# Eight of a batch's sixteen rows of B through DMA and ScalarE instead of TensorE, and a second product with C on GpSimd

## The reference, cut to what matters

```python
xn = layernorm(x)
deltaBC = xn @ W_deltaBC.T                       # 64 + 16 + 16 columns
delta, Bmat, Cmat = split(deltaBC)
delta = softplus(delta @ W_dt.T + b_dt)          # [b, 512, 256]
deltaA = exp(delta[..., None] * A)               # [b, 512, 256, 16]
BX = delta[..., None] * Bmat[:, :, None, :] * xn[..., None]
hs = scan(h = deltaA * h + BX, along the tokens)
y = einsum('blds,bls->bld', hs, Cmat) + D * xn
ffn = for each expert: gate * (gelu(xn[top] @ W1 + b1) @ W2 + b2), added to rows top
out = x + y + ffn
```

## Time and profile before

| What | Value |
|---|---|
| median of three runs | 2448.2 us |
| profiled execution | 2447.02 us, span 2445.2 us |
| VectorE busy | 2384.4 us (98%), 2042 instructions |
| TensorE matmuls busy | 2307.3 us (94%), 10748 instructions |
| GpSimd busy | 2127.3 us (87%), 1204 instructions |
| ScalarE busy | 1945.9 us (80%), 3374 instructions |
| DMA queues, share of 16 engines | 29.4% (SyncE's), 19.5% (GpSimd's) |
| granted TensorE clock | full speed in nearly all slices after the first tenth |

### The profile page before, as it was taken

How to read it: one execution, slowest core, us unless ns; L and a number is a source line. 1 busy time by engine, 2 the same in 40 slices (tenths; PEclk the granted TensorE clock), 3 DMA queues, 4 the chain that set the end, 5 groups by cost and what they waited for, 6 DMA issues and landing times. The chain is left out here.

```text
span 2445.2 us, 33085 instructions
## 1 busy us (share of the span) xinstructions
PE 2307.3 (94%) x10748; PEld 1812.6 (74%) x10748; DVE 2384.4 (98%) x2042; ACT 1945.9 (80%) x3374; POOL 2127.3 (87%) x1204
## 2 busy tenths in 40 slices
PE   7749999999999999999999999999999999999995
PEld 4427777777777777777777777777777777777774
DVE  6899999999999999999999999999999999999996
ACT  7747878788888888888888888878888888788873
POOL 4427999999999899999999999999999989999996
PEclk9969999999999999999999999999999999999997
DMA  9956464534445444444545354454545354454433
GB/s 343 336 202 222 131 186 130 152 95 134 118 120 139 117 129 112 135 118 100 156 102 152 96 144 103 113 137 120 141 107 139 99 143 110 112 145 105 97 103 52
DMA packets 120924, 335.87 MB, mean 137 GB/s; under 512 B 17488, under 2 KB 69808, under 8 KB 104112
## 3 DMA queue, kind: packets, MB, share of 16 engines
q1 hardware_dynamic: 65776, 249.60, 29.4%
q0 software_dynamic: 53760, 83.92, 19.5%
q10 hardware_dynamic: 1216, 0.23, 0.0%
HBM read 256.61 MB, written 91.75 MB: 142 GB/s over the span
## 5 line engine op out<-in xcount | busy, mean ns | idle before, releaser
L566 POOL TENSOR_TENSOR ysum<-ysum,prod 128x1024 f32<-128x1024 f32 x448 | 1198.7, 2676 | 55.1 <-DVE prod L971 46.0
L960 DVE TENSOR_TENSOR_SCAN bank_x<-decay,bank_x 128x1024 f32<-128x1024 f32 x480 | 1097.3, 2286 | 4.3
L1113 PE MATMUL bank_l<-ext,w_sb 128*128 128x256 f32 x4096 | 970.7, 382 | 52.4 <-ACT og L725 38.9
L1177 PE MATMUL bank_l<-w_sb,hid 128*128 128x256 f32 x4096 | 952.6, 383 | 0.0
L1113 PEld LDWEIGHTS bank_l<-ext,w_sb 128*128 128x128 f32 x4096 | 758.3, 191 | 203.6 <-ACT og L725 47.1
L1177 PEld LDWEIGHTS bank_l<-w_sb,hid 128*128 128x128 f32 x4096 | 762.7, 190 | 159.0 <-issue 52.5
L700 ACT ACTIVATE hid<-bank_l,b_all 128x256 f32<-128x256 f32 x1024 | 431.0, 474 | 372.7 <-PE bank_l L1113 372.3
L691 ACT ACTIVATE decay<-delta,a_sb 128x511 f32<-128x511 f32 x1024 | 640.2, 707 | 1.2
L902 DVE TENSOR_TENSOR bank_x<-du,bank_b 128x1024 f32<-128x1024 f32 x512 | 616.2, 1203 | 0.0
L971 DVE TENSOR_TENSOR prod<-bank_x,c_all 128x1024 f32<-128x1024 f32 x480 | 583.8, 1216 | 0.1
L522 POOL DMA_INDIRECT out<-og,idx_all x256 | 410.3, 1603 | 43.8 <-POOL ysum L566 38.2
(11 more groups left out here) (101 smaller groups left out, 1653.3 us busy)
## 6 DMA issues: line engine op xcount, KB each, us to landing
c_all<-bc_rows SPq DMA_DIRECT2D x128, 1024.0 KB, 5.1
w_sb<-in_w SPq DMA_DIRECT2D x32, 1024.0 KB, 10.6
decay<-in_x SPq DMA_DIRECT2D x32, 512.0 KB, 6.8
xn_rows<-c_all SPq DMA_DIRECT2D x32, 512.0 KB, 6.5
out<-yrow POOLq DMA_DIRECT2D x32, 512.0 KB, 6.3
xr<-xn_rows SPq DMA_DIRECT2D x30, 512.0 KB, 6.2
bc_rows<-prod SPq DMA_DIRECT2D x32, 192.0 KB, 5.1
rank<-bc_rows SPq DMA_DIRECT2D x32, 128.0 KB, 5.9
```

The source lines that it names most:

```text
L566: nc.gpsimd.tensor_tensor(ysum[:, m % 2], first, prod[:, i], ALU.add).then_inc(sum_done, 1)
L960: nc.vector.tensor_tensor_scan(into, decay[:, k % 2, i].rearrange("p c t -> p (c t)"), bank_x[:, s % 2], 0.0, ALU.mult, ALU.add).then_inc( ...
L1113: i = nc.tensor.matmul(bank_l[(q + v) % 2][:, (f % 2) * UT:(f % 2 + 1) * UT], w1_sb[:, e2, hc, f * P:(f + 1) * P], ext[:, v % 2, hc], star ...
L1177: i = nc.tensor.matmul(o, hid[:, w % 2, f, c * K:(c + 1) * K], w2_sb[:, w_par, f], start=False, stop=(f == FC - 1 and c == UB - 1))
```

## The change

GpSimd makes the products of steps 4 and 8. The scan of step 8 goes to a new SBUF tile `kept`, the product is made in place, and it is not added to `ysum`: `y_rows` transposes `kept` as a third term into the same bank. The scan of step 4 goes to `zabs` instead of the tile `state`, so ScalarE's `take_z`, which overwrites `zabs` for the next batch, waits for that product. Rows 4k+1 and 4k+2 of B (steps 1, 2, 5, 6, 9, 10, 13, 14) are loaded from `bc_rows` to all partitions by SyncE (`load_b_wide`, 512 KB a slot, one buffer) and copied into `bank_b` by ScalarE ahead of the gelus of pairs 0 and 2. TensorE spreads only rows 4k+3 and 4k+4. In TensorE's slot, the second expansion of delta (slot 2) and the first half of `y_rows` (slot 3) move from q = 0 to q = 1, behind up pair 0. `b_parts` moves into `yrow`'s memory.

```diff
-GP_STEP = 4
+GP_STEPS = (4, 8)
+KEPT = 8
+WIDE = (1, 2)
...
-        state = sb("state", [P, HC, T])
+        state = zabs
+        kept = sb("kept", [P, 2, HC, T])
+        b_wide = sb("b_wide", [P, len(WIDE), T])
...
         def sums(s):
-            return s - (s + N - 1) // N
+            return s - (s + N - 1) // N - (s + N - 1 - KEPT) // N
...
+            def load_b_wide(u):
+                held(b_ready, (u - 1) * STEPS + WIDE[-1] + 1)
+                first = R + u % SLOTS * STEPS + WIDE[0]
+                sp.dma_start(b_wide[:], bc_rows[u // SLOTS:u // SLOTS + 1, first:first + len(WIDE), :]
+                             .broadcast_to([P, len(WIDE), T])).then_inc(bw_in, 16)
...
+                    if there(u + 1, NU):
+                        load_b_wide(u + 1)
...
-                            if n == GP_STEP:
+                            if n in GP_STEPS:
                                 pool.wait_ge(scan_done, s + 1)
                                 pool.wait_ge(c_in[u % 2], (u // 2 + 1) * 16)
+                                from_, to = (kept[:, m % 2], kept[:, m % 2]) if n == KEPT else (state[:], prod[:, i])
...
-                            if n > 0:
+                            if n > 0 and n != KEPT:
                                 nc.gpsimd.tensor_tensor(ysum[:, m % 2], first, prod[:, i], ALU.add).then_inc(sum_done, 1)
...
+            def spread_b(s):
+                act.wait_ge(bw_in, (s // STEPS + 1) * 16)
+                act.wait_ge(bx_done, s)
+                nc.scalar.copy(bank_b[:], b_wide[:, s % STEPS - WIDE[0]]).then_inc(b_ready, 1)
...
+                        if there(u, NU) and pair in (0, 2):
+                            spread_b(u * STEPS + WIDE[pair // 2])
                         if there(v, NU):
                             gelus(v, v, pair)
...
-                        if n == GP_STEP:
-                            wait(dve, gp_prod_done, b)
+                        if n == KEPT:
+                            wait(dve, y_tr, b * 2 - 2)
+                            into = kept[:, par].rearrange("p c t -> p (c t)")
+                        elif n in GP_STEPS:
+                            dve.wait_ge(delta_done, b + 1)
...
-                        for term in (ysum, skip):
+                        for term in (ysum, kept, skip):
...
-                            if q % 2 == 0 and there(s + 1, NB * N):
+                            if q % 2 == 0 and (n + 1) % STEPS not in WIDE and there(s + 1, NB * N):
...
-                        if q == 0 and sl == 2 and there(b, NB) and there(b + 1, NB):
+                        if q == 1 and sl == 2 and there(b, NB) and there(b + 1, NB):
...
-                        if q == 0 and 0 < b < NB and sl == y_slot(b):
+                        if q == 1 and 0 < b < NB and sl == y_slot(b):
```

More of the change, by code:

```diff
@@ L124, in build @@
         zabs = sb("zabs", [P, HC, T])
-        state = sb("state", [P, HC, T])
+        state = zabs
+        kept = sb("kept", [P, 2, HC, T])
         yrow = sb("yrow", [P, 2, TC, D])
         rank = sb("rank", [R, T])
-        b_parts = sb("b_parts", [P, 3, 2, T], BF16)
+        b_wide = sb("b_wide", [P, len(WIDE), T])
         bcs = sb("bcs", [3 * 2 * N, 2, T], BF16)
@@ L141, in build @@
         xtr = delta[:, :, :, :]
+        b_parts = yrow[:, :, :, :].rearrange("p a c d -> p (a c d)")[:, 0:3 * T].bitcast(BF16).rearrange(
+            "p (a g t) -> p a g t", a=3, g=2)
         hflat = hid[:, :, :, :].rearrange("p a f t -> p (a f t)")
@@ L237, in build @@
         b_ready = sem("b_ready")
+        bw_in = sem("bw_in")
         c_in = [sem(f"c_in{i}") for i in range(2)]
@@ L263, in sums @@
         def sums(s):
-            return s - (s + N - 1) // N
+            return s - (s + N - 1) // N - (s + N - 1 - KEPT) // N
         def gp_prods(s):
-            return (s + N - 1 - GP_STEP) // N
+            return sum((s + N - 1 - n) // N for n in GP_STEPS)
         def dve_prods(s):
@@ L397, in _ @@
             load_c(0)
+            load_b_wide(0)
             for g in range(2, NG):
@@ L549, in main @@
                         if there(b, NB):
-                            if n == GP_STEP:
+                            if n in GP_STEPS:
                                 pool.wait_ge(scan_done, s + 1)
                                 pool.wait_ge(c_in[u % 2], (u // 2 + 1) * 16)
+                                from_, to = (kept[:, m % 2], kept[:, m % 2]) if n == KEPT else (state[:], prod[:, i])
                                 wait(pool, sum_done, sums(s - 2))
-                                nc.gpsimd.tensor_tensor(prod[:, i], state[:], c_all[:, u % 2, i][:, None, :].broadcast_to([P, HC, T]),
+                                nc.gpsimd.tensor_tensor(to, from_, c_all[:, u % 2, i][:, None, :].broadcast_to([P, HC, T]),
                                                         ALU.mult).then_inc(gp_prod_done, 1)
-                                pool.wait_ge(gp_prod_done, b + 1)
+                                pool.wait_ge(gp_prod_done, gp_prods(s + 1))
                             else:
@@ L656, in take_yrow @@
                 act.wait_ge(y_tr, y * 2 + half + 1)
+                if y == 0 and half == 0:
+                    for g in range(2):
+                        act.wait_ge(parts_out[g], NG // 2 * 48)
                 wait(act, y_added, (y - 1) * 16)
@@ L663, in take_z @@
                 wait(act, delta_done, nb - 1)
+                wait(act, gp_prod_done, gp_prods((nb - 2) * N + KEPT) if nb > 1 else 0)
                 wait(act, du_done, nb - 2)
@@ L897, in multiply_b @@
                 dve.wait_ge(du_done, b + 1)
-                if (s - 2) % N == GP_STEP:
+                if (s - 2) % N in GP_STEPS:
                     wait(dve, scan_done, s - 1)
@@ L1135, in main @@
                                 spread_b(s + 1, (n + 1) % N, m % 2 if n < N - 1 else (m + 1) % 2)
-                        if q == 0 and sl == 2 and there(b, NB) and there(b + 1, NB):
+                        if q == 1 and sl == 2 and there(b, NB) and there(b + 1, NB):
                             pe.wait_ge(z_taken, b * 4 + 6)
                             expand(b + 2, 1)
-                        if q == 0 and 0 < b < NB and sl == y_slot(b):
+                        if q == 1 and 0 < b < NB and sl == y_slot(b):
                             pe.wait_ge(sum_done, sums(b * N))
+                            pe.wait_ge(gp_prod_done, gp_prods(b * N))
                             pe.wait_ge(skip_done, b)
@@ L1194, in main @@
                             pe.wait_ge(sum_done, sums(NB * N))
+                            pe.wait_ge(gp_prod_done, gp_prods(NB * N))
                             pe.wait_ge(skip_done, NB)
```

## The result

The changed kernel takes 2457.5 us (median of five runs, 2453.72 to 2461.69), the kernel before 2447.8 us (five runs). The ratio is 1.0043, with a 95% interval of 1.0029 to 1.0057: slower by 0.43%, some 10 us. The prediction had 2453 us, a range of 2434 to 2468, and 0.45 for slower. The profiled execution took 2453.72 us, with a span of 2451.9.

The account below looks back on a forecast made before the run. VectorE bounds the kernel before, the chain through TensorE and ScalarE to row 1 after: 32 x 0.16 = 5.1 us over the profiled 2447.0, plus about 1 us at the end, gives 2453 us; range 2434 to 2468.

Parts of the forecast that it names:

- What bounds the kernel: Main stage: VectorE, busy 99.8%, sets the pace before; after the change, the chain through row 1, chance 0.58.
- VectorE's saving at step 8: Step 8 on VectorE loses its product: 4.45 - 3.53 = 0.92 us a batch.
- The copy of row 1 is late: Slot 0, step 1: ScalarE's copy into `bank_b` comes 0.16 us late by VectorE's present clock; VectorE waits 1.08 us.
- What TensorE gains on the way: TensorE from row 8 to row 15: fewer spreads and waits, more transposes, gaining 0.33 + 0.53 + 0.52 = 1.38 us.
- rival B: Slot 3: ScalarE's copy of row 13 delays the gelus of pair 0, up pair 2 waits; about 2474 us, chance 0.16.
- the sign that this wait is gone: Changed kernel's trace, slot 3: TensorE's wait for the gelus of pair 0, 0.48 us, should be gone.
- The batch: Main stage: one batch takes 70.13 + 0.16 = 70.29 us.
- The term of 0.16 us a batch: Copy of row 1: 1.54 us late less 1.38 gained by TensorE; 32 x 0.16 = 5.1 us in all.
- Rival A: ScalarE's copy of row 1 is in time; GpSimd sets 69.76 us: 2435, or 2418 without the gather's 0.63; chance 0.24.
- GpSimd's 69.76: GpSimd's own need a batch: 70.13 - 1.0 slack + 0.63 for the gather's wait at step 8 = 69.76 us.
- Rival C: GpSimd's added product blocks VectorE, 2.36 us a batch: 75 us less the saving of 29, so 2493; chance 0.02.
- The chain does not contain the saving: The chain leaves VectorE at step 7 and returns at step 1, so step 8's 0.92 us only makes VectorE wait longer.

## Why the prediction was right

- **What bounds the kernel.** Right. VectorE set the pace before; the changed kernel's is set by a chain through three engines that ends at row 1, as forecast.
- **VectorE's saving at step 8.** Forecast 0.92 us a batch, measured 4.44 - 3.53 = 0.91.
- **The copy of row 1 is late.** Forecast: VectorE waits 1.08 us at step 1, released by ScalarE's copy. Measured: 1.05, 29 times in 2000 us. The copy takes 0.60 us (forecast 0.62), and VectorE starts 0.62 us behind its start, where I had 0.72.
- **What TensorE gains on the way.** Forecast 0.33 + 0.53 + 0.52 = 1.38 us. Measured: at row 8 0.33 (0.39 late before, 0.06 now), from row 8 to row 11 13.96 - 13.53 = 0.43, from row 12 to row 15 13.06 - 12.67 = 0.39. Together 1.15. In slot 2 the 0.1 too little is the up pair that now stands ahead of the expansion: the expansion starts 1.82 us after it (1269.22 to 1271.04), where half of two pairs in a row is 1.73 ((1220.21 - 1216.75) / 2 in the earlier trace rows). In slot 3 it is up pair 2, which meets the gelus of pair 0 about as they end: rival B's mechanism, at a small part of its price. The two up pairs take 3.84 us there, where two in a row took 3.62 before, so the sign that this wait is gone came true only in part.
- **The batch.** 70.29 was forecast, 70.46 measured. Of the 0.17 between them 0.13 is TensorE's 0.23 (1.38 forecast, 1.15 measured) less the 0.10 that the handover was quicker, and the rest lies in the steps behind the wait. Row 10 also came just late (step 9 is 0.07 long), where I had 0.3 us of room; this lies inside the stretch from step 7 to step 1, so it only shortened the wait at step 1. The term of 0.16 us a batch measured 0.33. The mechanism was right, its small remainder was twice what I had, and 2453 became 2457.5. That remainder was the difference of 1.54 and 1.38, two sums of estimates, and the misses in them partly cancelled: that it came so close is in part luck.
- **Rival A.** Did not happen: ScalarE was late. What it would have given is shown by row 1 on TensorE: with that copy out, 2422.8 us, between the 2418 and the 2435 of the rival. The pace is then VectorE's own and not GpSimd's 69.76. What I had wrong in that term is mainly the gather behind the product: forecast 0.8 us of idle ahead of it, measured 0.27. That is 0.52 of the 0.76 us between 69.76 and the estimate of 69.0; the rest I can't place.
- **Rival C.** Did not happen. VectorE's scans take 2.27 to 2.30 us after as before. The Trainium skill (Perfetto Trace Analysis, Optimizing Scalar/DVE Operations) says that moving work between VectorE and GpSimd might not help because they share a read port; no operation of VectorE here became longer for it (the multiplications by `du` take 1.21 us in the mean, before 1.20), and the move gained 10 us in the kernel without copies.
- **"The chain does not contain the saving."** Only two thirds right. Giving it back costs 0.33 of 0.91 us, through a second chain that leaves VectorE behind step 8, at the multiplication of step 15.

## What to carry to other kernels

An engine with 20% of idle time isn't free at every moment: ask of each piece of work that is moved to it when it arrives there and by when the result is wanted. With one buffer between two engines the window is short (3.2 us here), and the one copy out of eight that stands behind the longest unbroken stretch of work sets the time for all. When a saving is made on the pacing engine, look for chains that leave it and return without passing the saving, and count how far behind the next such chain is before saying that the saving is worth nothing or all.

## What the runs showed of the hardware that was not expected

- A copy from SBUF to PSUM of 128x512 f32 on ScalarE took 0.60 us, like one from PSUM to SBUF (0.58 to 0.60), and one from SBUF to SBUF without a scale 0.61; two that follow each other start 0.50 us apart.
- A semaphore wait of VectorE costs a little more than its idle time: where it waited 1.05 us the step grew by 1.17. Without a wait the next instruction starts about 0.1 us before the last one's recorded end (2.19 us after a scan of 2.29).
- The gather on GpSimd right behind a product of its own that it waits for has 0.27 us of idle ahead of it, the gather of step 0, which waits for the same number of semaphores, 0.79. Why they differ stays open.
